# A linear-attention layer and six local-attention layers on one core: mask written by ScalarE, low part of the projection input on GpSimd, new slot order

## The reference, cut to what matters

```python
qkv = x @ Wqkv                       # 128 -> 3 * 1024, 16 heads of 64
q = l2norm(q) * qs;  k = l2norm(k) * ksc
q = q * cos * scale + rotate_half(q) * sin * scale      # k with 1 / scale
sim = einsum('bhwie,bhwje->bhwij', bq, bk2) * 8.0       # windows of 32 queries, 64 keys
mask = (it < jb) | (it > jb + w) | (jb == -1)
sim = where(mask, -finfo.max, sim);  attn = softmax(sim, -1)
x = (attn @ v) @ Wo + x
xn = layernorm(x) * g + bln
x = (a * gelu(gate)) @ W2 + b2 + x   # a, gate = split(xn @ W1 + b1)
```

## Time and profile before

| what | us |
|---|---|
| median of 3 runs | 3747.72 (3747.24 to 3754.5) |
| profiled execution | 3743.95 |
| its span | 3742.1 |
| TensorE busy | 3470.4 |
| DVE busy | 3141.4 |
| ScalarE busy | 2271.7 |
| GpSimd busy | 1852.4 |
| ten steady rounds (442.42 to 785.72) | 343.30 |

### The profile page before, as it was taken

One profiled execution on the slowest core, in us unless ns is written; L12 is line 12 of the kernel. 1 busy time (PEld: TensorE's weight loads), 2 busy tenths in 40 slices (PEclk: granted clock), 3 DMA queues, 4 the chain that ended last, 5 costly groups with the idle time before them and its releaser, 6 DMA issues.

```text
span 3742.1 us, 161812 instructions
## 1 busy us (share of the span) xinstructions
PE 3470.4 (93%) x63907; PEld 2773.6 (74%) x63907; DVE 3141.4 (84%) x6016; ACT 2271.7 (61%) x4159; POOL 1852.4 (50%) x1604
## 2 busy tenths in 40 slices
PE   5758999999999999999999999999999999999996
PEld 2326787877788878788878788877788887788784
DVE  8987888888788888788888788888788888888883
ACT  2014666666666666666666666666566666666663
POOL 2435455454554554545554445545455445455541
PEclk9988999999999999999999999999999999999998
DMA  2002423323333323333223333232432332332332
GB/s 84 9 28 50 104 60 70 77 54 78 91 67 77 72 56 80 82 77 77 64 64 76 85 77 71 57 77 67 95 72 59 73 77 54 79 74 60 70 77 73
DMA packets 186363, 261.00 MB, mean 70 GB/s; under 512 B 31670, under 2 KB 89908, under 8 KB 185396
## 3 DMA queue, kind: packets, MB, share of 16 engines
q1 hardware_dynamic: 186164, 258.24, 30.7%
HBM read 22.30 MB, written 4.19 MB: 7 GB/s over the span
## 4 chain that ended last, share of the span: by engine, by line
PE 71%; issue 13%; DVE 7%; POOL 3%; ACT 3%; SPq 2%; DMA 1%; ACTq 0%; POOLq 0%; DVEq 0%
PE bank L653 9%; PE bank L705 8%; PE bank L637 7%; PE bank L613 6%; PE obank L687 6%; PE bank L738 5%; PE bank L615 4%; PE bank L614 4%; PE bank L697 4%; PE bank L663 4%; PE bank L745 3%; DVE xs_lo L1139 3%; PE bank L647 2%; PE bank L628 2%; PE bank L630 2%
## 5 line engine op out<-in xcount | busy, mean ns | idle before, releaser
L951 POOL TENSOR_TENSOR qn<-qn,rinv 128x512 f32<-128x512 f32 x768 | 805.4, 1065 | 1382.1 <-DVE rinv L1198 1382.1
L945 POOL TENSOR_TENSOR qn<-ropec,ropes 128x512 f32<-128x512 f32 x768 | 982.9, 1294 | 274.6 <-DVE ropes L1150 230.8
L1149 DVE TENSOR_TENSOR ropec<-bank,rots 128x512 f32<-128x512 f32 x768 | 526.7, 686 | 116.0 <-ACT sq L833 63.7
L1158 DVE TENSOR_REDUCE ss<-sq 128x8 f32<-128x512 f32 x768 | 513.2, 679 | 88.0 <-ACT sq L833 82.6
L1150 DVE TENSOR_TENSOR ropes<-bank,rots 128x512 f32<-128x512 f32 x768 | 523.7, 682 | 0.0
L833 ACT ACTIVATE sq<-bank 128x512 f32<-128x512 f32 x768 | 448.8, 598 | 87.7 <-PE bank L615 68.9
L855 ACT ACTIVATE Pr<-Pr 128x512 f32<-128x512 f32 x384 | 241.9, 630 | 399.1 <-DVE Pr L1209 396.9
L637 PE MATMUL bank<-ident,qn 128*128 128x128 f32 x3072 | 464.1, 274 | 18.4 <-POOL qn L951 14.9
L653 PEld LDWEIGHTS bank<-kT,qT 64*32 64x32 f32 x24576 | 363.1, 107 | 122.0 <-issue 121.9
L613 PE MATMUL bank<-wqkv_hi,xs_hi 128*128 128x512 f32 x768 | 353.1, 460 | 99.2 <-DVE xs_lo L1139 90.8
L637 PEld LDWEIGHTS bank<-ident,qn 128*128 128x128 f32 x3072 | 375.9, 141 | 83.9 <-issue 18.8
(11 more groups left out here) (137 smaller groups left out, 6215.9 us busy)
## 6 DMA issues: line engine op xcount, KB each, us to landing
V<-Vt SPq DMA_DIRECT2D x576, 260.0 KB
V<-Vt SPq DMA_DIRECT2D x192, 130.0 KB
V<-Vt SPq DMA_DIRECT2D x192, 65.0 KB
xres<-X SPq DMA_DIRECT2D x96, 128.0 KB
X<-x SPq DMA_DIRECT2D x96, 128.0 KB, 2.0
wqkv_raw<-L_ffn_Wqkv SPq DMA_DIRECT2D x6, 1536.0 KB
xraw<-X SPq DMA_DIRECT2D x97, 64.0 KB
xraw<-X SPq DMA_DIRECT2D x97, 63.8 KB
```

Source lines behind the costliest of these rows:

```text
L945: pool.tensor_tensor(qn[:, c, :], ropec[:, c % ROPE_RING, :], ropes[:, c % ROPE_RING, :], ALU.add).then_inc(rope_sum.sem, 1)
L951: pool.tensor_tensor(heads8(qn[:, c, :]), heads8(qn[:, c, :]), rinv[:, 8 * c:8 * c + 8].unsqueeze(2).broadcast_to([P, 8, DH]), ALU.mult).t ...
L1149: dve.tensor_tensor(halves(ropec[:, c % ROPE_RING, :]), raw, table(t, 2 * kind), ALU.mult)
L1158: dve.tensor_reduce(ss[:, 8 * c:8 * c + 8], heads8(sq[:, c % 2, :]), AX.X, ALU.add).then_inc(ss_done.sem, 1)
```

## The change

Three things change. The first projection input's low part, xs_lo, moves from DVE to GpSimd, in the same form. The mask is no longer written by TensorE but by ScalarE, as a copy of the float32 mask, spread over eight heads, into the bank (`mk`, 128x512); TensorE waits for it and adds all 32 products onto it. One mask matmul stays, once, in front of the pipeline (`sim_begun`). And the table ORDER is another one for all four engines.

```diff
@@ ORDER
     "pe": """
-        tr.0' pt.2'' w1.0''' pv.1'' proj.0 proj.1 tr.1' ot.0'' w1.1''' tr.2' pv.2'' pt.3'' tr.3' proj.2
+        pv.1'' tr.0' w1.0''' ot.0'' tr.1' proj.0 proj.1 pv.2'' tr.2' pt.3'' w1.1''' tr.3' proj.2 proj.3
...
     "pool": """
-        norm.4' norm.5' add.0 add.1 norm.6' add.2 add.3 norm.7' add.4 norm.0 add.5 norm.1 norm.2 norm.3
-        add.6 add.7 """,
+        norm.1' xs.0 norm.2' norm.3' norm.4' norm.5' norm.6' norm.7' add.0 add.1 add.2 add.3 add.4 add.5
+        add.6 norm.0 add.7 """,
@@ TensorE
+            pe.matmul(b_sim[:], identb[:], maskb[:, 0, :].unsqueeze(1).broadcast_to([P, 8, 2 * WIN]),
+                      start=True, stop=True).then_inc(sim_begun, 1)
...
-                pe.wait_ge(sim_shift.sem, sim_shift.at(b, u) if u else sim_shift.at(b - 1, 4))
-
-                pe.matmul(b_sim[:], identb[:], maskb[:, 1 if t else 0, :].unsqueeze(1).broadcast_to([P, 8, 2 * WIN]),
-                          start=True, stop=False, skip_group_check=True)
+                hold(pe, pe_held, mask_put.sem, mask_put.at(b, u + 1))
@@ ScalarE
+            act.wait_ge(sim_begun, 1)
+
+            def b_mk(b, u):
+                act.wait_ge(sim_shift.sem, sim_shift.at(b, u) if u else sim_shift.at(b - 1, 4))
+                act.activation(heads8(b_sim[:]), mask_f[:, u // 2, :].unsqueeze(1).broadcast_to([P, 8, 2 * WIN]),
+                               ACT.Copy).then_inc(mask_put.sem, 1)
@@ GpSimd
+            def a_xs(a, _):
+
+                pool.wait_ge(xs_hi_done.sem, xs_hi_done.at(a, 1))
+                pool.tensor_tensor(xs_lo[:], xraw[:], xs_hi[:].bitcast(F32), ALU.subtract).then_inc(xs_lo_done.sem, 1)
@@ DVE
-            def a_xs(a, _):
-
-                dve.wait_ge(xs_hi_done.sem, xs_hi_done.at(a, 1))
-                dve.tensor_tensor(xs_lo[:], xraw[:], xs_hi[:].bitcast(F32), ALU.subtract).then_inc(xs_lo_done.sem, 1)
```

More of the change, by code:

```diff
@@ L52 @@
     "pe": """
-        tr.0' pt.2'' w1.0''' pv.1'' proj.0 proj.1 tr.1' ot.0'' w1.1''' tr.2' pv.2'' pt.3'' tr.3' proj.2
-        proj.3 tr.4' ot.1'' w1.2''' tr.5' pv.3'' proj.4 ot.2'' tr.6' w2.0''' ot.3'' tr.7' proj.5 proj.6
-        qk.0' wo.0'' qk.1' proj.7 v.0 mean.0'' pt.0' qk.2' var.0'' pt.1' pv.0' qk.3' v.1 v.2 ln.0'' v.3 """,
+        pv.1'' tr.0' w1.0''' ot.0'' tr.1' proj.0 proj.1 pv.2'' tr.2' pt.3'' w1.1''' tr.3' proj.2 proj.3
+        tr.4' ot.1'' w1.2''' tr.5' pv.3'' proj.4 tr.6' w2.0''' tr.7' ot.2'' proj.5 proj.6 ot.3'' qk.0'
+        wo.0'' qk.1' proj.7 v.0 mean.0'' pt.0' qk.2' pv.0' var.0'' pt.1' v.1 v.2 pt.2' v.3 ln.0'' qk.3' """,
     "act": """
-        tr.0' xs.0 wa.1 wa.2 qk.3'' w1.0''' pt.2'' proj.0 tr.1' ot.0'' proj.1 w1.1''' tr.2' pt.3'' tr.3'
-        proj.2 proj.3 tr.4' ot.1'' tr.5' w1.2''' wc.2''' ot.2'' proj.4 tr.6' tr.7' ot.3'' proj.5 proj.6
-        qk.0' x1.0'' wc.0'' proj.7 qk.1' v.0 pt.0' mean.0'' qk.2' v.1 pt.1' v.2 ln.0'' wc.1'' v.3 wc.3''' """,
+        pt.2'' xs.0 wa.1 wa.2 tr.0' qk.3'' w1.0''' proj.0 tr.1' ot.0'' proj.1 tr.2' pt.3'' w1.1''' tr.3'
+        proj.2 proj.3 tr.4' ot.1'' w1.2''' wc.2''' tr.5' proj.4 tr.6' tr.7' mk.0' ot.2'' proj.5 ot.3''
+        proj.6 mk.1' qk.0' x1.0'' wc.0'' proj.7 mk.2' v.0 pt.0' qk.1' mean.0'' qk.2' pt.1' v.1 v.2 mk.3' v.3
+        ln.0'' wc.1'' wc.3''' """,
     "dve": """
-        qk.3'' xs.0 wa.1 wa.2 pv.1'' w1.0''' proj.0 proj.1 sums.0 sums.1 pv.2'' w1.1''' proj.2 proj.3 sums.2
-        w1.2''' sums.3 pv.3'' proj.4 sums.4 w2.0''' sums.5 proj.5 sums.6 qk.0' proj.6 x1.0'' qk.1' sums.7
+        wa.1 wa.2 qk.3'' pv.1'' w1.0''' sums.0 proj.0 proj.1 sums.1 w1.1''' pv.2'' proj.2 sums.2 w1.2'''
+        proj.3 sums.3 proj.4 w2.0''' pv.3'' sums.4 proj.5 qk.0' sums.5 sums.6 proj.6 x1.0'' qk.1' sums.7
         mean.0'' proj.7 qk.2' var.0'' rsqrt.0 pv.0' ln.0'' """,
     "pool": """
-        norm.4' norm.5' add.0 add.1 norm.6' add.2 add.3 norm.7' add.4 norm.0 add.5 norm.1 norm.2 norm.3
-        add.6 add.7 """,
+        norm.1' xs.0 norm.2' norm.3' norm.4' norm.5' norm.6' norm.7' add.0 add.1 add.2 add.3 add.4 add.5
+        add.6 norm.0 add.7 """,
 }
@@ L201, in build @@
         const_in = sem("const_in")
+        sim_begun = sem("sim_begun")
         x_in_sem = [sem(f"x_in_{k}") for k in range(4)]
@@ L251, in build @@
         max_done = per_batch("max_done", 4)
+        mask_put = per_batch("mask_put", 4)
         sim_shift = per_batch("sim_shift", 4)
@@ L894, in c_ln_ @@
                 act.activation(xn[:], lnt[:], ACT.Identity, bias=vec[:, 1:2], scale=vec[:, 0:1]).then_inc(c_xn.sem, 1)
-            steps = {"xs": a_xs, "proj": a_proj, "v": a_v, "tr": a_tr, "qk": b_qk,
+            steps = {"xs": a_xs, "proj": a_proj, "v": a_v, "tr": a_tr, "mk": b_mk, "qk": b_qk,
                      "pt": b_pt, "ot": b_ot, "x1": c_x1_, "mean": c_mean, "ln": c_ln_,
@@ L953, in a_norm @@
                                    ALU.mult).then_inc(normed.sem, 1)
-            steps = {"add": a_add, "norm": a_norm}
+            def a_xs(a, _):
+                pool.wait_ge(xs_hi_done.sem, xs_hi_done.at(a, 1))
+                pool.tensor_tensor(xs_lo[:], xraw[:], xs_hi[:].bitcast(F32), ALU.subtract).then_inc(xs_lo_done.sem, 1)
+            steps = {"xs": a_xs, "add": a_add, "norm": a_norm}
             pool.wait_ge(x1_saved, 16)
@@ L1252, in c_w2 @@
                 dve.scalar_tensor_tensor(x2[:], b_c[:, 0:T], vec[:, 2:3], x1[:], ALU.add, ALU.add).then_inc(c_x2.sem, 1)
-            steps = {"xs": a_xs, "proj": a_proj, "sums": sum_squares, "rsqrt": rsqrt_, "qk": b_qk,
+            steps = {"proj": a_proj, "sums": sum_squares, "rsqrt": rsqrt_, "qk": b_qk,
                      "pv": b_pv, "x1": c_x1_, "mean": c_mean,
```

1 line of the change is left out of this document (added).

## The result

The changed kernel takes 3727.34 us (median of four runs, 3723.95 to 3729.13), beside 3747.48 us for the kernel before on the same chip (3745.54 to 3754.5): a ratio of 0.9942, 95% interval 0.9925 to 0.9959. It is faster by 0.6%, where 2.3% was forecast. The time lies inside the predicted range and the sign is right, but the size is a quarter of the forecast: 20 us, not 86. The profiled executions agree: spans of 3742.1 and 3722.1 us.

A forecast was written before the change was run, and what follows sets the result against it. TensorE's instruction stream was taken to set the round. Steps of 12.9 + 4.7 + 15.75 gave 33.3 us; 96 us saved less 10 at layer changes gave 86, so 3658, plus 3.8 for the median: 3662 us, range 3600 to 3735.

The forecast's parts named there:

- t = 0 to rinv: From the end of the first score group to the last reciprocal root: 12.9 us, against 13.02 before.
- the cover at mask 2: Scores 2 could start at 7.20 us, TensorE reaches them at 7.24: cover 0.04 us, the thinnest of the change.
- rinv to the first projection: TensorE's ln, scores 3, P·V 1, transposes and w1.0 put the first projection 4.7 us after rinv (R).
- The wait for ln: New TensorE wait of 0.3 us ahead of ln, since v.3 no longer stands behind ln.
- First projection to the next t = 0: Rest of the round, to the next first score group's end: 15.75 us, against 16.53 before.
- the removed 0.67 us: TensorE's wait for xs_lo before a round's first projection, taken to leave if xs_lo on GpSimd is covered.
- The contention: DVE's two-input xs_lo contends with GpSimd's norms reading SBUF: median 1320 ns against a minimum of 426.
- TensorE's side: Four 0.32 us mask matmuls leave, entry to small tiles costs 0.1 per score group; floor of the round 32.58 us.
- The round: Steady round of 33.3 us against 34.33, the floor plus 0.7 us of new waits; 96 us saved over 96 rounds.
- Layer changes: DVE's two long weight differences ahead of shift 3 delay ScalarE's exponential and gelu: 2 us x 5 = 10 charged.
- C: Rival: the mask's slot isn't freed, the array drains before small tiles load; round 33.9 us, 3707 us, chance 0.21.
- D: Slower rival: ScalarE's masks leave handoffs between DVE's shift and TensorE's scores bare; round 34.9 us, 3800 us, chance 0.09.

The follow-up runs named there:

- e3: Changed kernel with only TensorE's loop end moved, to between v.3 and ln: 3683.11 us, ratio 0.9835 against the kernel before.

## Why the prediction was right in direction and wrong in size

- **t = 0 to rinv**: predicted 12.9 us, measured 12.79 (1056.25 to 1069.04). Right. So is the mask at 0.598 us (0.60 taken), the cover at mask 2, and the absence of waits ahead of scores 1 and 3: 4.7 us in 8 waits over the whole run.
- **rinv to the first projection** is the step that failed: "R + 4.7", measured R + 5.27 (1069.04 to 1074.31). Its terms, each by spacing: ln to scores 3 0.64, where 0.44 was taken; scores 3 to P·V 1 1.63, where 1.13 was taken; P·V 0.78 (0.79); tr.0 to the projection 2.16 (2.18). The 0.5 us is the loop's end, a term that the walk put at nothing without a reason, although it knew the order to begin the list with P·V 1. Its three other positions show it, and e3, which moves nothing else, gives 44 us of the missing 66 back. The other 0.2 us stands between ln's transposes and scores 3 in e3 too (1064.79 to 1065.43). Half of it is the entry of 0.1 to small tiles, which the walk counted into the scores' 1.13; the other half is ln's transposes themselves, 0.71 us long instead of 0.60 (where a mask matmul follows them, in the kernel with the masks back on TensorE, they still take 0.55 instead of 0.44).
- **The wait for ln**, predicted 0.3, is 0.27 between v.3's last matmul and ln. Right.
- **First projection to the next t = 0**: predicted 15.75, measured 15.83. Right, though the gelu is done at R + 6.80 (1075.84) and not at R + 6.05.
- **xs_lo** takes 0.74 us on GpSimd (0.65 taken) and is covered, as said. What the prediction had wrong is its worth: it let the removed 0.67 us count for the move, but with xs_lo on DVE the new order has the same round. It was the order that covered it. The contention that it named is real, but it hangs on the moment: the same subtraction took 0.42 us a few steps later on DVE, with GpSimd's norms under it as well.
- **TensorE's side**: the entry of 0.1 and so a gain of 0.2 for each of masks 0 to 2 are borne out (0.12, 0.09, 0.09 us of entry).
- **The round**: 33.3 predicted, 33.89 measured. 0.59 times 96 are 57 us of the missing 66.
- **Layer changes**: "I charge 2 us x 5 = 10". Beyond steady rounds, the 25 rounds cost 943.12 - 25 x 34.33 = 85 us before and 953.26 - 25 x 33.89 = 106 after: 21. That is 11 more than charged. The prediction charged it to the weight differences, and there it was wrong about the place. In the first full round, where they stand, TensorE waited 6.29 us for xs_lo before and waits 4.08 for On 1 now, and the round lies 8.2 us above a steady one before and 7.8 after (means over the five changes). What grew is the third round and the fourth, from 2.3 to 6.0 and from 5.1 to 6.6 us above a steady round. TensorE's waits of 1 us or more marked issue sum to 11.5 us in the 25 rounds before and 25.7 after, and the granted clock of the first such third round is 0.90 after (886.48 to 927.09, in the windows above) and was 0.99 before:

```profile
898.17:935.07 36.90, 33.31 (x658) 27.37 (x658) 29.32 (x59) 24.53 (x51) 20.97 (x20) 0.99 0.32 69
```

  By the experiment with 64 more instructions such stalls lie at places of the code, and the change moved all the code; that this is the whole of it isn't shown. The differences ahead of On 1 still cost 13 to 24 us that can be had back (by the medians, and by the profiled rounds, of e3 and the kernel with them moved back).
- **The rivals**: C gave the measured round, 33.9 us, for a wrong reason. By its mechanism, an array that drains before small tiles load, the scores would start 0.3 us late in front of every group; they start 0.1 late in front of groups 0 to 2 and 0.2 in front of group 3, and putting the masks back costs 0.55 us a round. A forecast that meets a number by another mechanism isn't confirmed by it. D doesn't occur in the new order and does in the old, where it costs over 5%, most of it while the granted clock is low.

The two repairs, the loop closed between v.3 and ln and the weight differences moved back, give 3670 us, against the 3662 forecast. Its round is 33.42, a tenth above the 33.3. That the sum then nearly meets the forecast doesn't make the forecast's layer changes right.

## What to carry to other kernels

The end of a loop is an entry in each engine's order like any other: when you reorder, write it into the list, price it, and put it where the engine has a few long instructions in hand, or must wait anyway, and not behind many short ones. A wait that goes when work is moved to another engine says nothing yet of the move's worth: here neither move gained anything in the old order, one of them nothing in the new order's steady round, and the order with xs_lo's move nothing without the masks'. The price of an instruction read in one place need not hold in another: look at what it ran beside, and when. And a chain that passes through a second engine needs independent work between its two ends, since a bare handoff costs its own length, and in some rounds here a slower clock followed.
